# Linear attention on one core: scores and values as fp16 halves, three fp16 products for one fp32 product

## The chip, the core and the metric

The kernel runs on one NeuronCore of a Trainium2 chip. The core has a matrix engine (PE, TensorE), a vector engine (DVE), an activation engine (ACT, ScalarE), a general one (POOL, GpSimd), a queue that issues transfers (SP), an on-chip memory (SBUF, 128 partitions) and an accumulator memory for PE's results (PSUM, eight banks of 128x512 fp32). The metric is the device time of one execution in microseconds (us), as the median of some runs.

## The reference

A transformer block of six sublayers over `x` of 8 sequences x 512 tokens x 256 features in fp32. The second sublayer is the one that matters here, gated linear attention (GLA) with 4 heads, keys of 64 and values of 128 features:

```
x = x + 0.5 * ffn(layernorm(x))            # mixture of experts
x = x + gla(layernorm(x))                  # the sublayer that is changed
x = x + 0.5 * ffn(layernorm(x))
x = x + 0.5 * ternary_ffn(layernorm(x)); x = x + window_attn(layernorm(x)); x = x + 0.5 * ternary_ffn(layernorm(x))

# gla: q, k, g: [B, H, N, 64], v: [B, H, N, 128], g = log decay <= 0
S_t = diag(exp(g_t)) S_{t-1} + k_t v_t^T ;  o_t = q_t^T S_t
o = o * rsqrt(mean(o * o) + 1e-5) * rms_w
return (o.reshape(B, N, 512) * silu(x @ Wg.T)) @ Wout.T
```

## The kernel before

**Tiling.** A sequence of 512 tokens is four chunks of 128 (TPS = 4). Within a chunk the recurrence becomes a masked product: scores `att` = k q^T with the decays multiplied into q and k, masked causally, times the values. Across chunks it is a state per head, 64x128, that DVE carries on. The output of a chunk is att·v plus q·state, both accumulated in one PSUM region. Four heads are two pairs `p` of two heads `h`; half `j` of the sequence is chunks 2j and 2j+1. PE's fp16 matmuls elsewhere run in threes (`mm3`, L1701 to L1703): a value is held as an upper fp16 half and a lower fp16 half, and hi·hi, hi·lo and lo·hi are added up.

**Order.** Each engine runs a program of its own, in order; semaphores tie them. In `gla` each has a `body(g)` for sequence g; `each_sequence(..., True)` runs sequences 0 to 5 as a loop of three iterations of two, and 6 and 7 written out. PE's body: scores (L2006), transposes of the keys (L2014), the projections of the next sequence (`low`, `keys`, `logits`: L1701 to L1703 and L1978), key-value products for the states (L2030, `kt` as the stationary operand), then chunk by chunk att·v (L2042, fp32, 128 rows) and q·state (L2047, fp32, 64 rows), then the next sequence's queries and cumulated decays (L1991), the gates, the values, the turns of the gated output (L2065) with the transposes of the next rows (L1717) between them, and the output product.

**The others, around the change.** DVE masks the scores of each half from PSUM into `m.att` (L1571), then does the logits of the next sequence (L1517, L1521), the chain of states (L1562, L1565), decay (L1527), sums of squares (L1584), and the gated product (L1592). ACT copies the turned keys (L979), the low-rank rows (L949) and the keys of the next sequence (L952), does softplus (L956 to L960), the squares (L986), queries (L965), exps (L970), gates (L993), values (L975) and the upper half of the turned output (L997). PE's L2030 waits for L979, for the values and for L952, because its results go into the banks of the keys. POOL adds eps to the mean squares and raises them to -1/2 (L734, L736), scales the gates (L741), and issues an accumulating DMA of expert rows (`second_rows`, L663). `m.squares` is the same memory as `m.att`. `w1q` and `w2q` are weight buffers of a later sublayer. Before the first body, the engines work through sequence 0's projections; PE's first transposes there (L1717) wait for ACT's exps (L970).

Of the kernel before, what the change touches and what calls it, by code (L numbers as in the profile page):

```python
# [105 lines left out]
def build(nc, T, out):  # L106

    ctx = ExitStack()
    with ctx:
# [12 lines left out]
        def const(name):  # L122
            return consts[:, const_at(name)]
# [44 lines left out]
        eps = sb("eps", [P, TPS])  # L168
# [40 lines left out]
        halves_set = sem("causal_and_ones_in_half_precision")  # L209
# [18 lines left out]
        for n, kind in enumerate(SUBLAYERS):  # L228
# [7 lines left out]
                "gla": "stacked t_ready t_hi t_lo qk_ready qk_copied logits_ready lb_ready soft_step g_ready v_ready v_copied "  # L236
                       "kt_ready kt_copied cum_ready exps_ready f_step q_ready k_ready at_ready masked st_ready s_step "
                       "gate_ready gate_done gate_scaled o_ready sq_ready ss_ready orstd_step orstd_ready og_ready ogt_ready "
                       "ogt_hi ogt_lo y_ready y_taken",
                "win": "zeroed padded qk_ready qk_copied v_ready v_copied v_out v_in0 v_in1 sc_ready mx_ready "  # L240
                       "sub_ready exp_ready sum_ready rl_ready norm_ready pt_ready pt_copied c_ready ct_hi ct_lo y_ready "
                       "y_taken bias_hi bias_lo bias_product bias_row centred windowed bias_added",
# [155 lines left out]

        def gla_space():
# [16 lines left out]
            m.squares = m.att  # L416
            m.o_hi, m.o_lo = at([2, 2, 2, GPAIR, P], F16), at([2, 2, 2, GPAIR, P], F16)
# [3 lines left out]

        def flat(a):

            return a.rearrange("p a b c d -> p (a b c d)") if len(a.shape) == 5 else a.rearrange("p a b c -> p (a b c)")
# [217 lines left out]
        def _(pool):  # L642
            nc.gpsimd.memset(neghalf[:], -0.5).then_inc(rstd_step, 1)
            nc.gpsimd.memset(eps[:], EPS).then_inc(rstd_step, 1)
            pool.wait_ge(rstd_step, 2)

            def rstd_of(m):

                pool.wait_ge(mv_ready, m + 1)
                nc.gpsimd.tensor_tensor(rstd[:], mv[:, :, 1], eps[:], ALU.add).then_inc(rstd_step, 1)  # L650
# [75 lines left out]
            def gla(n):  # L726
                s, m = S[n], gla_space()
                work_left(n)

                def body(g):  # L730
                    if not is_last(g):
                        rstd_of(g + N0(n) + 2)
                    pool.wait_ge(s["ss_ready"], g * 2 + 2)
                    nc.gpsimd.tensor_tensor(m.orstd, m.ss, eps[:, 0:1, None].broadcast_to([P, 2, TPS * H // 2]), ALU.add).then_inc(s["orstd_step"], 1)  # L734
# [8 lines left out]
                    if g + 3 < NSEQ:  # L743
                        second_rows(n - 1, g + 3)

                second_rows(n - 1, 2)
                for g in range(NSEQ):
                    body(g)

            def win(n):  # L750
# [35 lines left out]
                def step(g, u):  # L786
# [10 lines left out]
                    if is_first(g):  # L797
                        pool.wait_ge(s["bias_row"], 1)
# [24 lines left out]
        def _(act):  # L823
# [120 lines left out]
            def gla(n):  # L944
                s, m = S[n], gla_space()

                def low_keys(g):
# [14 lines left out]
                def queries(g):  # L962
                    for p in range(GPAIR):
                        act.wait_ge(s["qk_ready"], g * 2 * GPAIR + GPAIR + p + 1)
                        nc.scalar.activation(m.q[:, p], ps[:, GQ[p], :], ACT.Copy, scale=DK ** -0.5 / WS).then_inc(s["qk_copied"], 1)  # L965
# [1377 lines left out]
```

## Time and profile before

| | us |
|---|---|
| median of 3 runs (1719.59 to 1725.48) | 1723.2 |
| the profiled execution | 1716.48 |
| its span, first to last instruction | 1714.4 |
| PE busy | 1638.2 (96%) |
| DVE busy | 1146.9 (67%) |
| ACT busy | 858.2 (50%) |
| POOL busy | 671.4 (39%) |
| granted TensorE clock, mean | 0.989 |

The profile is of one execution. A row of its timeline gives start, duration, engine, line of kernel.py, operation, written tile <- read tiles, shapes and how many instructions are merged into it; in square brackets, how long the engine had been idle and what ended that. A matmul's duration includes its way through the array, so matmuls overlap: what a stream costs is read from starts, or from the difference of two groups. An fp32 matmul shows as two instructions. PEld is PE's weight load, which runs beside the matmuls.

### The profile page before, as it was taken

The numbers are of one execution on the slowest core, as the hardware profiler recorded it, in microseconds if no ns is written. First come the engines' busy times: TensorE is split into PE (matmuls) and PEld (weight loads), VectorE is DVE, ScalarE is ACT, GpSimd is POOL, SyncE is SP. The second block draws the span as 40 slices with busy tenths as digits, with TensorE's granted clock in tenths as the row PEclk, the third lists the DMA queues.
The fourth block names the chain that finished last, engine by engine and source line by source line (L and its number), as shares of the span: only waits on it lengthen the run. The fifth ranks groups of instructions, "written<-read, shape, count | busy, mean of one in ns | idle before, by whom it ended". The sixth has DMA issues, their size and how long they took to land.

```text
span 1714.4 us, 41995 instructions
## 1 busy us (share of the span) xinstructions
PE 1638.2 (96%) x14962; PEld 1106.0 (65%) x14963; DVE 1146.9 (67%) x2505; ACT 858.2 (50%) x1474; POOL 671.4 (39%) x652
## 2 busy tenths in 40 slices
PE   6999999999989999999999999999999989998999
PEld 3665656666567776765565656666566767777666
DVE  6677766666556666656766656666677678776675
ACT  4455434444466555644343334444466566564774
POOL 2342333444122222123342333444244488888243
PEclk9999999999999999999999999999999999998999
DMA  7132323333302111002210123333322033221011
GB/s 249 53 110 84 97 85 98 110 106 104 84 13 38 24 25 24 1 1 84 87 50 26 37 75 96 111 108 101 96 63 48 2 76 77 54 62 40 14 37 50
DMA packets 90149, 115.69 MB, mean 67 GB/s; under 512 B 9296, under 2 KB 76400, under 8 KB 90032
## 3 DMA queue, kind: packets, MB, share of 16 engines
q1 hardware_dynamic: 69680, 71.17, 14.8%
q0 software_dynamic: 20352, 42.88, 8.8%
q8 instruction: 83, 1.36, 0.3%
q14 instruction: 34, 0.28, 0.1%
HBM read 66.11 MB, written 47.90 MB: 67 GB/s over the span
## 4 chain that ended last, share of the span: by engine, by line
PE 81%; DVE 7%; POOL 4%; ACT 4%; issue 3%; DMA 2%; SPq 0%; DVEq 0%; ACTq 0%; POOLq 0%
PE ps L1701 18%; PE ps L1703 18%; PE ps L1702 18%; PE ps L1944 3%; PE ps L1945 3%; PE ps L1717 3%; PE ps L2042 2%; PE ps L1925 2%; PE ps L1926 2%; PE ps L1863 2%; PE ps L1882 2%; PE ps L2199 2%; PE ps L2181 1%; PE ps L2169 1%; PE ps L2047 1%
## 5 line engine op out<-in xcount | busy, mean ns | idle before, releaser
L719 POOL DMA_INDIRECT routed<-work x142 | 136.5, 961 | 234.5 <-DVE work L1456 229.4
L1701 PE MATMUL ps<-later_hi,work 128*128 (+1 forms) x632 | 203.0, 321 | 1.2 <-ACT work L1054 1.0
L1702 PE MATMUL ps<-later_lo,work 128*128 (+1 forms) x632 | 203.0, 321 | 0.0
L1703 PE MATMUL ps<-later_hi,work 128*128 (+1 forms) x632 | 202.9, 321 | 0.0
L1701 PE MATMUL ps<-xt_hi,wsh 128*128 128x512 f16 x512 | 195.1, 381 | 5.3 <-DVE work L1344 3.0
L1702 PE MATMUL ps<-xt_lo,wsh 128*128 128x512 f16 x512 | 195.0, 381 | 0.0
L1703 PE MATMUL ps<-xt_hi,wsh 128*128 128x512 f16 x512 | 194.9, 381 | 0.0
L864 ACT ACTIVATE work<-ps 128x512 f32<-128x512 f32 x128 | 76.4, 597 | 182.4 <-PE ps L1703 182.1
L650 POOL TENSOR_TENSOR rstd<-mv,eps 128x4 f32<-128x4 f32 x49 | 14.7, 300 | 385.9 <-DVE mv L1149 375.1
L1701 PE MATMUL ps<-wsh,work 128*128 128x256 f16 x512 | 140.3, 274 | 4.0 <-ACT work L853 2.7
L1703 PE MATMUL ps<-wsh,work 128*128 128x256 f16 x512 | 140.4, 274 | 0.0
L1702 PE MATMUL ps<-wsh,work 128*128 128x256 f16 x512 | 140.3, 274 | 0.0
L1344 DVE SCALAR_TENSOR_TENSOR work<-ps,work 128x512 f32<-128x512 f32 x128 | 88.0, 689 | 73.7 <-ACT work L864 68.7
L1443 DVE SCALAR_TENSOR_TENSOR work<-ps,work 128x256 f32<-128x256 f32 x142 | 68.7, 484 | 98.4 <-ACT work L906 98.4
L933 ACT ACTIVATE work<-ps,cols 128x512 f32<-128x512 f32 x128 | 88.0, 687 | 64.5 <-PE ps L1926 46.3
L906 ACT ACTIVATE work<-ps 128x256 f32<-128x256 f32 x142 | 54.5, 384 | 130.4 <-PE ps L1703 128.6
L1482 DVE TENSOR_TENSOR work<-work 128x512 f16<-128x512 f32 x128 | 86.9, 716 | 43.8 <-ACT work L926 42.5
L1945 PE MATMUL ps<-w2q,work 128*128 128x256 f16 x512 | 113.3, 273 | 0.0
L1944 PE MATMUL ps<-w2q,work 128*128 128x256 f16 x512 | 113.3, 273 | 0.0
L1925 PE MATMUL ps<-xt_hi,w1q 128*128 128x512 f16 x256 | 98.1, 383 | 6.0 <-DVE xt_lo L1164 6.0
L842 ACT ACTIVATE xt_hi<-ps 128x1024 f16<-128x1024 f32 x49 | 50.1, 1023 | 101.8 <-PE ps L1717 101.8
L1926 PE MATMUL ps<-xt_lo,w1q 128*128 128x512 f16 x256 | 98.0, 383 | 0.0
(247 smaller groups left out, 4234.2 us busy)
## 6 DMA issues: line engine op xcount, KB each, us to landing
work<-expert_x SPq DMA_DIRECT2D x142, 129.0 KB, 2.1
yg<-in_w_later SPq DMA_DIRECT2D x9, 496.0 KB, 3.5
w1q<-in_w_later SPq DMA_DIRECT2D x9, 496.0 KB, 3.7
yg<-in_w SPq DMA_DIRECT2D x8, 512.0 KB, 3.6
values<-wsh SPq DMA_DIRECT2D x8, 512.0 KB, 3.3
later_hi<-values SPq DMA_DIRECT2D x16, 256.0 KB, 4.6
later_lo<-values SPq DMA_DIRECT2D x16, 256.0 KB, 4.7
out_x<-x SPq DMA_DIRECT2D x8, 512.0 KB, 3.0
```

The source lines that it names most:

```text
L719: nc.gpsimd.indirect_dma_start(routed[:, :], bass.IndirectOffsetOnAxis(m.homes[:, i:i + 1], 0), m.t_y[:, i % 4, :], None).then_inc(s[f"til ...
L864: nc.scalar.activation(m.silu[:, k % 2, :], ps[:, up_bank(g, k), :], ACT.Silu, scale=1 / WS).then_inc(s["silu_ready"], 1)
L933: nc.scalar.activation(relu[:, k % RELUS, :], ps[:, 2 + k % 4, :], ACT.Relu, bias=b1_col[:, k:k + 1]).then_inc(s["relu_ready"], 1)
L1344: nc.vector.scalar_tensor_tensor(out=m.prod[:, k % PRODS, :], in0=ps[:, up_bank(g, k) + 1, :], scalar=HS / WS, in1=m.silu[:, k % 2, :], op ...
L1482: nc.vector.tensor_tensor(h_lo[:, u, k, :], relu[:, k % RELUS, :], h_hi[:, u, k, :], ALU.subtract).then_inc(s["h_lo_ready"], 1)
L1701: nc.tensor.matmul(out_, a[0], b[0], start=start, stop=False)
L1702: nc.tensor.matmul(out_, a[0], b[1], start=False, stop=False)
L1703: return nc.tensor.matmul(out_, a[1], b[0], start=False, stop=stop)
L1925: nc.tensor.matmul(ps[:, 2 + q % 4, :], w, xt_hi[:, u, k, TOK], start=(k == 0), stop=False)
L1926: ins = nc.tensor.matmul(ps[:, 2 + q % 4, :], w, xt_lo[:, u, k, TOK], start=False, stop=(k == KT - 1))
L1944: nc.tensor.matmul(o, h_hi[:, u, q, sl], w, start=(q == 0), stop=False)
L1945: ins = nc.tensor.matmul(o, h_lo[:, u, q, sl], w, start=False, stop=(q == FU - 1))
```

## The change

After masking, the scores are split: ACT casts them to fp16 (`upper_scores`, into `a_hi`), and POOL subtracts that from the fp32 scores and writes the rest as fp16 (`a_lo`). The values are split in the same way (`upper_values` on ACT, `lower_values` on POOL), into `w1q` and `w2q`. For memory, DVE now writes the masked scores of half 0 into the room of half 1, and those of half 1 into `xn` (in the last sequence `m.lb`); the halves of j=1 are written over the fp32 scores of j=0, so ACT's cast of half 1 waits until POOL has done with half 0. On ACT the cast of half 0 stands at the head of the body, that of half 1 between the copies of the low-rank rows and the keys, and that of the next values at its end (for sequence 0 ahead of the exps). On POOL the two subtractions stand at the head of the body and that of the next values at its end. PE does, for each half, all att·v products (three of fp16 for one of fp32), waiting on `half_lo`, and then all q·state products. Queries and values are scaled by HS = 16, and eps of the output norm by HS to the fourth. Some semaphores of other sublayers are joined (`stacked`, `bias_hi` into `halves_set`; `bias_lo` into `bias_row`), which leaves their waits as they were.

```diff
+            spare = xn[:, :, 0:D]
+            rooms = [flat(m.att[:, j]) for j in range(2)]
+            m.whole = lambda g, j: (m.lb if is_last(g) else spare) if j else rooms[1].rearrange("p (a d) -> p a d", d=D)
+            halves = [a.bitcast(F16) for a in rooms]
+            m.a_hi, m.a_lo = ([a[:, n * TPS * D:(n + 1) * TPS * D].rearrange("p (h c a t) -> p h c a t", h=2, c=2, a=GPAIR)
+                               for a in halves] for n in range(2))
+            m.v_hi, m.v_lo = (a[:, :].rearrange("p (c d) -> p c d", c=TPS) for a in (w1q, w2q))
...
+                def lower_values(g):
+                    pool.wait_ge(s["half_hi"], g * 3 + 1)
+                    nc.gpsimd.tensor_tensor(m.v_lo, m.v, m.v_hi, ALU.subtract).then_inc(s["half_lo"], 1)
+
                 def body(g):
+                    for j in range(2):
+                        pool.wait_ge(s["half_hi"], g * 3 + 2 + j)
+                        nc.gpsimd.tensor_tensor(flat(m.a_lo[j]).rearrange("p (a d) -> p a d", d=D), m.whole(g, j),
+                                                flat(m.a_hi[j]).rearrange("p (a d) -> p a d", d=D), ALU.subtract).then_inc(s["half_lo"], 1)
...
                         second_rows(n - 1, g + 3)
+                    if not is_last(g):
+                        lower_values(g + 1)
 
                 second_rows(n - 1, 2)
+                lower_values(0)
...
                     act.wait_ge(s["t_ready"], g + 1)
                     nc.scalar.activation(m.t[0:3 * LOW], ps[0:3 * LOW, GLOW, :], ACT.Copy, scale=1 / WS).then_inc(s["t_hi"], 1)
+                    if between is not None:
+                        between()
                     for p in range(GPAIR):
...
+                def upper_values(g):
+                    act.wait_ge(s["v_copied"], (g + 1) * TPS)
+                    nc.scalar.activation(m.v_hi, m.v, ACT.Copy).then_inc(s["half_hi"], 1)
+
+                def upper_scores(g, j):
+                    act.wait_ge(s["masked"], g * 2 + j + 1)
+                    if j:
+                        act.wait_ge(s["half_lo"], g * 3 + 2)
+                    nc.scalar.activation(flat(m.a_hi[j]).rearrange("p (a d) -> p a d", d=D), m.whole(g, j), ACT.Copy).then_inc(s["half_hi"], 1)
 
                 def body(g, u):
+                    upper_scores(g, 0)
                     act.wait_ge(s["kt_ready"], g + 1)
...
                     if not is_last(g):
-                        low_keys(g + 1)
+                        low_keys(g + 1, lambda: upper_scores(g, 1))
                         softplus(g + 1)
+                    else:
+                        upper_scores(g, 1)
...
                     turned_hi(1)
+                    if not is_last(g):
+                        upper_values(g + 1)
...
                 queries(0)
+                upper_values(0)
                 exps(0)
...
                     for j in range(2):
                         dve.wait_ge(s["at_ready"], g * 2 + j + 1)
-                        nc.vector.tensor_tensor(flat(m.att[:, j]).rearrange("p (a t) -> p a t", t=P),
-                                                ps[:, 2 * j:2 * j + 2, :].rearrange("p a (b t) -> p (a b) t", t=P),
-                                                const("causal")[:, None, :].broadcast_to([P, 2 * H, P]), ALU.mult).then_inc(s["masked"], 1)
+                        if j:
+                            dve.wait_ge(pt_ready, g + N0(n) + 2)
+                        nc.vector.tensor_tensor(m.whole(g, j).rearrange("p a (b t) -> p a b t", t=P),
+                                                ps[:, 2 * j:2 * j + 2, :].rearrange("p a (b c t) -> p (a b) c t", t=P, b=2),
+                                                const("causal")[:, None, None, :].broadcast_to([P, H, 2, P]), ALU.mult).then_inc(s["masked"], 1)
...
-                    for c in range(TPS):
-                        if c % 2 == 0:
-                            pe.wait_ge(s["masked"], g * 2 + c // 2 + 1)
-                        if c:
+                    for j in range(2):
+                        pe.wait_ge(s["half_lo"], g * 3 + 2 + j)
+                        for c in range(2 * j, 2 * j + 2):
+                            for p in range(GPAIR):
+                                for h in range(2):
+                                    own = slice((2 * p + h) * DV, (2 * p + h + 1) * DV)
+                                    a, v = (m.a_hi[j], m.a_lo[j]), (m.v_hi, m.v_lo)
+                                    for ah, vh in ((0, 0), (0, 1), (1, 0)):
+                                        nc.tensor.matmul(ps[:, 2 * j + h, block(c, h, p)], a[ah][:, h, c % 2, p], v[vh][:, c, own],
+                                                         start=c == 2 * j and p == ah == vh == 0, stop=False, skip_group_check=True)
+                        for c in range(max(2 * j, 1), 2 * j + 2):
                             pe.wait_ge(s["s_step"], g * 5 + 2 * c - 1)
-                        for p in range(GPAIR):
-                            for h in range(2):
-                                ins = nc.tensor.matmul(ps[:, c // 2 * 2 + h, block(c, h, p)], m.att[:, c // 2, h, c % 2, p],
-                                                       m.v[:, c, (2 * p + h) * DV:(2 * p + h + 1) * DV], start=True, stop=c == 0)
-                            if c:
+                            for p in range(GPAIR):
                                 for h in range(2):
                                     rows_ = slice(h * DK, (h + 1) * DK)
-                                    ins = nc.tensor.matmul(ps[:, c // 2 * 2 + h, block(c, h, p)], m.q[rows_, p, c * P:(c + 1) * P],
-                                                           m.states[rows_, c - 1, p], start=False, stop=True)
-                        if c % 2:
-                            ins.then_inc(s["o_ready"], 1)
+                                    ins = nc.tensor.matmul(ps[:, 2 * j + h, block(c, h, p)], m.q[rows_, p, c * P:(c + 1) * P],
+                                                           m.states[rows_, c - 1, p], start=False,
+                                                           stop=c == 2 * j + 1 and p == GPAIR - 1, skip_group_check=True)
+                        ins.then_inc(s["o_ready"], 1)
```

## Rows read from the trace of the kernel before

**Rows 1.** The page: busy us of each engine, share of the span, instructions.

```profile
PE 1638.2 (96%) x14962; PEld 1106.0 (65%) x14963; DVE 1146.9 (67%) x2505; ACT 858.2 (50%) x1474; POOL 671.4 (39%) x652
```

**Rows 2.** The waits of PE, 490 to 775 us: who waited <- for whom: total us, times, longest.

```profile
PE ps L2030 <- ACT work L952: 1.8, 7, 0.3
```

**Rows 3.** The timeline of PE, L2030 of two sequences: start us, us, engine, line, operation, tiles, count.

```profile
607.75 1.53 PE L2030 MATMUL ps<-work 128*64 128x128 f32 x24 [0.25 <-ACT work L952]
...
646.62 1.53 PE L2030 MATMUL ps<-work 128*64 128x128 f32 x24 [0.25 <-ACT work L952]
```

**Rows 4.** The timeline of PE, the scores, values and turns of one sequence.

```profile
600.32 2.06 PE L2006 MATMUL ps<-work 64*128 64x128 f32 x32
...
609.21 1.60 PE L2042 MATMUL ps<-work 128*128 128x128 f32 x12
610.75 0.49 PE L2047 MATMUL ps<-work 64*128 64x128 f32 x4
611.17 0.71 PE L2042 MATMUL ps<-work 128*128 128x128 f32 x4
...
616.49 0.39 PE L1701 MATMUL ps<-xt_hi,later_hi 128*128 128x512 f16 x1
616.71 0.38 PE L1702 MATMUL ps<-xt_lo,later_hi 128*128 128x512 f16 x1
...
629.93 1.04 PE L2065 MATMUL ps<-consts,work 128*128 128x128 f32 x8
```

**Rows 5.** The timeline of PE near 189 us: fp16 matmuls of 256 columns, then of 8.

```profile
188.91 0.27 PE L1703 MATMUL ps<-wsh,work 128*128 128x256 f16 x1
189.02 0.27 PE L1701 MATMUL ps<-wsh,work 128*128 128x256 f16 x1
...
189.40 0.17 PE L1703 MATMUL ps<-wr_hi,xt_lo 128*128 128x8 f16 x1
189.43 0.17 PE L1701 MATMUL ps<-wr_hi,xt_hi 128*128 128x8 f16 x1
```

**Rows 6.** The timeline of ACT, the same sequence: the copies behind PE's products.

```profile
603.21 0.81 ACT L979 ACTIVATE work<-ps 128x768 f32<-128x768 f32 x1 [7.01 <-PE ps L2014]
...
605.80 0.60 ACT L952 ACTIVATE work<-ps 128x512 f32<-128x512 f32 x1 [0.70 <-PE ps L1703]
607.10 0.60 ACT L952 ACTIVATE work<-ps 128x512 f32<-128x512 f32 x1 [0.70 <-PE ps L1703]
```

**Rows 7.** The page's groups: a cast on ACT; busy us and mean ns after the bar.

```profile
L926 ACT ACTIVATE work<-work 128x512 f16<-128x512 f32 x128 | 78.9, 632 | 0.0
```

**Rows 8.** The timeline of DVE, 480 to 770 us: the masking of three sequences.

```profile
601.53 2.35 DVE L1571 TENSOR_TENSOR work<-ps,consts 128x1024 f32<-128x1024 f32 x2 [0.29 <-PE ps L2006]
...
640.74 2.35 DVE L1571 TENSOR_TENSOR work<-ps,consts 128x1024 f32<-128x1024 f32 x2 [0.63 <-PE ps L2006]
...
757.10 2.35 DVE L1571 TENSOR_TENSOR work<-ps,consts 128x1024 f32<-128x1024 f32 x2 [0.41 <-PE ps L2006]
```

**Rows 9.** The timeline of POOL, the same sequence: the power and the scaling.

```profile
621.62 2.94 POOL L736 TENSOR_TENSOR work<-work,neghalf 128x16 f32<-128x16 f32 x1
625.67 3.76 POOL L741 TENSOR_TENSOR work<-work 128x1024 f32<-128x1024 f32 x2 [1.12 <-ACT work L993]
```

**Rows 10.** The timeline of ACT and PE at the first sequence.

```profile
476.89 1.94 ACT L970 ACTIVATE work<-ps 128x1024 f32<-128x1024 f32 x2
...
478.92 1.58 PE L1717 MATMUL ps<-consts,xn 128*128 128x128 f32 x8 [2.85 <-issue]
```

**Rows 11.** Busy time by stretch, first sequence: PE, PEld, DVE, ACT, POOL, clock, DMA share, GB/s.

```profile
481.50:486.70 5.20, 5.12 (x40) 4.83 (x41) 3.67 (x3) 1.45 (x3) 0.00 (x0) 0.55 0.01 3
```

**Rows 12.** The timeline of all engines at the last sequence.

```profile
758.79 0.81 ACT L979 ACTIVATE work<-ps 128x768 f32<-128x768 f32 x1 [7.01 <-PE ps L2014]
...
759.70 1.53 PE L2030 MATMUL ps<-work 128*64 128x128 f32 x24 [0.95 <-issue]
```

**Rows 13.** One line's instructions on POOL, another sublayer: ns least, median, most.

```profile
L675 POOL TENSOR_TENSOR x<-x,rows x64: 716/727/2312, 1232.2 to 1701.6; 128x256 f32<-128x256 f32 x64
```

More of the change, by code:

```diff
@@ L167, in build @@
         tsum, thr = sb("tsum", [P, 2, 2]), sb("thr", [P, 2, 2])
-        eps = sb("eps", [P, TPS])
+        eps = sb("eps", [P, TPS + 1])
         neghalf = sb("neghalf", [P, 4 * TPS])
@@ L397, in l1ffn_space, with flat @@
             return r([2, FU, SEQ], F16), r([2, FU, SEQ], F16), r([RELUS, SEQ])
+        def flat(a):
+            return a.rearrange("p a b c d -> p (a b c d)") if len(a.shape) == 5 else a.rearrange("p a b c -> p (a b c)")
         def gla_space():
@@ L643, in _ @@
             nc.gpsimd.memset(neghalf[:], -0.5).then_inc(rstd_step, 1)
-            nc.gpsimd.memset(eps[:], EPS).then_inc(rstd_step, 1)
+            nc.gpsimd.memset(eps[:, 0:TPS], EPS)
+            nc.gpsimd.memset(eps[:, TPS:], EPS * HS ** 4).then_inc(rstd_step, 1)
             pool.wait_ge(rstd_step, 2)
@@ L649, in rstd_of @@
                 pool.wait_ge(mv_ready, m + 1)
-                nc.gpsimd.tensor_tensor(rstd[:], mv[:, :, 1], eps[:], ALU.add).then_inc(rstd_step, 1)
+                nc.gpsimd.tensor_tensor(rstd[:], mv[:, :, 1], eps[:, 0:TPS], ALU.add).then_inc(rstd_step, 1)
                 pool.wait_ge(rstd_step, m + 3)
@@ L733, in body @@
                     pool.wait_ge(s["ss_ready"], g * 2 + 2)
-                    nc.gpsimd.tensor_tensor(m.orstd, m.ss, eps[:, 0:1, None].broadcast_to([P, 2, TPS * H // 2]), ALU.add).then_inc(s["orstd_step"], 1)
+                    nc.gpsimd.tensor_tensor(m.orstd, m.ss, eps[:, TPS:, None].broadcast_to([P, 2, TPS * H // 2]), ALU.add).then_inc(s["orstd_step"], 1)
                     pool.wait_ge(s["orstd_step"], g + 1)
@@ L964, in queries @@
                         act.wait_ge(s["qk_ready"], g * 2 * GPAIR + GPAIR + p + 1)
-                        nc.scalar.activation(m.q[:, p], ps[:, GQ[p], :], ACT.Copy, scale=DK ** -0.5 / WS).then_inc(s["qk_copied"], 1)
+                        nc.scalar.activation(m.q[:, p], ps[:, GQ[p], :], ACT.Copy, scale=HS * DK ** -0.5 / WS).then_inc(s["qk_copied"], 1)
                 def exps(g):
@@ L974, in values @@
                         act.wait_ge(s["v_ready"], g * TPS + c + 1)
-                        nc.scalar.activation(m.v[:, c], ps[:, banks[c], :], ACT.Copy, scale=1 / WS).then_inc(s["v_copied"], 1)
+                        nc.scalar.activation(m.v[:, c], ps[:, banks[c], :], ACT.Copy, scale=HS / WS).then_inc(s["v_copied"], 1)
+                def upper_values(g):
[6 more added lines that the diff above has]
+                    nc.scalar.activation(flat(m.a_hi[j]).rearrange("p (a d) -> p a d", d=D), m.whole(g, j), ACT.Copy).then_inc(s["half_hi"], 1)
                 def body(g, u):
+                    upper_scores(g, 0)
                     act.wait_ge(s["kt_ready"], g + 1)
@@ L1071, in step @@
                                 values_rows(g + 1)
-                nc.scalar.activation(m.bv[0], bv_col, ACT.Copy).then_inc(s["bias_hi"], 1)
+                nc.scalar.activation(m.bv[0], bv_col, ACT.Copy).then_inc(halves_set, 1)
                 queries_keys(0, 0, range(2 * KT))
```

24 lines of the change are left out of this document (11 added, 13 removed).

## The prediction

> **What bounds the kernel now.** The page comes first: PE is busy 96% of the span, the next engine 67% [rows 1]. The gated linear attention (GLA) sublayer is even tighter: the waits of PE show one a sequence there, 0.3 us, for ACT's last key copy at L952 [rows 2], and the eight sequences follow each other every 38.87 us (L2030 at 607.75 and 646.62) [rows 3]. So a microsecond taken from PE's row of matmuls here is a microsecond of the kernel, as long as ACT, POOL and DVE deliver earlier by as much. The timeline of PE shows what is edited: between 609.21 and 616.49, 7.28 us, run the fp32 attention-times-values products (L2042) and the query-times-state products (L2047), alternating in fours [rows 4]. The timelines of the other engines then show what stands on either side of it.
>
> **PE's part: what is removed.** One fp32 matmul is two instructions. A group of 12 at L2042 takes 1.60 us and one of 4 takes 0.71, so one pass costs 0.89 / 8 = 0.111. The 64-row passes run two at a time: 32 of them (L2006) take 2.06, 4 (L2047) take 0.49, so one costs 1.57 / 28 = 0.056 [rows 4]. The 7.28 us hold 32 x 0.111 = 3.55 and 24 x 0.056 = 1.34. The other 2.39 fall on 12 changes between full and 64-row shapes (the ones at both ends counted as one each), 0.20 each.
>
> **PE's part: what is added.** 48 fp16 matmuls of 128 columns, each with a weight load. No such shape is in the trace. At 256 columns they start 0.11 apart, which is 256 columns at the granted 2.4 GHz (0.107) and 0.003; at 8 columns they start 0.03 apart, so load and issue together need at most that [rows 5]. For 128 columns this gives 0.0565 with the load hidden and 0.053 + 0.030 = 0.083 with it exposed. I take 0.0565, since the 256-column rows hide it. The order by kind leaves 4 shape changes. New stretch: 48 x 0.0565 + 24 x 0.056 + 4 x 0.20 = 2.71 + 1.34 + 0.80 = 4.85. PE gains 7.28 - 4.85 = 2.43 a sequence, and 1.1 with exposed loads.
>
> The Trainium skill ("TensorE: Matmul & The Clock Gate", section "Back-to-back issue gap") gives about 81 ns a matmul for a stream of loads and matmuls at 128 columns, and that would leave PE about 1.2 us of gain a sequence. The same sentence gives 131 ns for 512 columns, where this trace shows 0.22 us (616.49 to 616.71) [rows 4].
>
> **The new chain ahead of PE.** DVE masks half j=0, ACT casts it to fp16, POOL subtracts to get the lower half, and only then may ACT cast j=1, because that cast overwrites the fp32 scores of j=0. In ACT's queue the cast of j=1 stands ahead of both key copies, for which PE waits already.
> - Mask j=0: two masks take 2.35 us from 601.53, so the first ends at about 602.7 [rows 8].
> - ACT's cast of 1024 elements: from PSUM 512 take 0.60 and 768 take 0.81 [rows 6], 0.84 ns an element; 512 from SBUF to fp16 take 0.63 [rows 7]. So 1.05. It ends at 603.8 and pushes the copy at L979 from 603.21 to 603.8, which no one is near.
> - POOL's subtraction: its 1024-element TENSOR_TENSOR takes 1.9 (two in 3.76) [rows 9]. No mixed fp16 and fp32 one is shown; I take 1.9, with 1.3 and 2.9 as bounds. It ends at 605.8.
> - ACT's cast j=1: 605.85 to 606.9. The key copies then run 606.9 to 607.5 and 607.4 to 608.0, where they now run from 605.80 and 607.10 [rows 6]. PE starts L2030 at 608.05 instead of 607.75: **0.3 lost**.
> - Sequences 2 and 4, which begin a loop iteration: DVE's mask starts 0.34 later against PE (640.74 against 601.53 plus 38.87) [rows 8]; 0.65 lost.
> - Sequence 0 loses nothing, since PE's slower clock there spreads the work that covers the chain [rows 11].
>
> The second POOL subtraction runs 607.0 to 608.9, and PE needs it at about 611.9: hidden, 3 us to spare. The casts of the values (ACT 2048 elements, 1.9 us; POOL 3.8) run at about 596.3 to 602.1, where ACT is idle for 7 us [rows 6] and POOL idle; they are over 1.7 us before POOL gets the scores. If POOL were 1.5 times as slow, that cover would be gone. Softplus starts at 608.64, after the key copies, so DVE's and POOL's chains behind it stay where they are. The changed eps, the scale factors and the renamed semaphores cost nothing: the same instructions, or one memset at the start beside the loads.
>
> **What is late next.** POOL's power ends at 621.62 + 2.94 = 624.56, tied to softplus. Its scaling (1.9) would end at 626.5, DVE's product (1.2) at 627.7, and PE's first turn at L2065 is at 629.93 [rows 4, 9]. With 2.1 us gained PE comes at 627.8, just in time. So no sequence gains more than about **2.1**.
>
> **The last sequence** has no projections of a next one behind which to hide. The mask starts at 757.10 [rows 8]; cast to 759.4, L979's copy ends at 760.2 instead of 759.6, and PE's L2030 moves from 759.70 to 760.25 [rows 12]. POOL's first half is done at 761.4, the second cast at 762.5, the second subtraction at 764.5. Then 24 products, one shape change and 16 passes, 1.35 + 0.2 + 0.9 plus the hand-over, end at about 767.0 against 768.44: **1.4 gained**.
>
> **The start.** ACT casts the values of sequence 0 ahead of its exps. These run 476.89 to 478.83 and PE has been waiting for them 2.85 us when it starts at 478.92 [rows 10]. The whole 1.9 us goes on the path. PE's granted clock in the stretch behind it is 0.55, so mostly the lower level, 1.2 GHz [rows 11]; a longer wait may lengthen that stretch. If 1.9 us more work fell into it, 0.9 would be lost, and if it ended at the same moment as now, 0.9 won. I take zero.
>
> **The sum.** Sequences 0, 1, 3, 5, 6: 5 x 2.1 = 10.5. Sequences 2 and 4: 2 x (2.43 - 0.65) = 3.5. Last: 1.4. Start: -1.9. Together **13.5 us**. The profiled execution took 1716.5 (span 1714.4 and 2.1 around it), so its like should take 1703.0. The median of the runs, 1723.2, lies 6.7 above it; I carry the difference over: 1709.7.
>
> **Rivals.**
> - *The weight loads show.* 0.083 a matmul instead of 0.0565: 48 x 0.0265 x 8 = 10.2 us less gain, 3.3 left, 1719.9. For it: no stream of this width is in the trace. Against: the 256-column stream hides them. Chance 0.13. By the 81 ns of the Trainium skill the loss would be 48 x 0.0245 x 8 = 9.4 us, and the time 1719.
> - *POOL's mixed subtraction is slower, 2.9 us.* It stands on the path: 1.0 each in sequences 1 to 6, 2.0 in the last, 8 us, leaving 5.5: 1717.7. For it: L675's instruction of a quarter of the size takes 0.73 in the median, not 0.5 [rows 13]. Chance 0.15.
> - *POOL takes double, and the kernel gets slower.* At 3.8 us, the values' subtraction (7.5) ends at 605.8 and holds back the scores' by 1.8, which itself costs 1.9 more: 3.7 x 6 and 5.6 in the last, 27.8 against 13.5: 1737.5. L675 shows POOL can be held up: 0.72 at least, 2.31 at most [rows 13]. Without the queue the loss is 8 x 1.9 x (f - 1) for a factor f; from f = 1.5 on the queue adds 26 x (f - 1.5), and the two together eat the gain at about f = 1.63, 3.1 us. Against: POOL's products at L741 hold at 1.9 [rows 9]. Chance 0.10. The Trainium skill ("SBUF — State Buffer", section "Who interferes with whom") says that a DVE instruction with two SBUF inputs and a GpSimd instruction that reads SBUF exclude one another. DVE's work beside the new subtractions (masking, L1517, L1521, L1602) reads PSUM and one SBUF tile, so by that rule f stays 1. The trace agrees as far as it goes: L675's long instances run beside DVE's L1482, which has two SBUF inputs.
> - *The forecast*, 0.62, own range 1705 to 1714.
>
> **Range and chances.** The range takes in the forecast and the first two rivals with some spread between runs, not the third: 1704 to 1722. A measurement of this kernel can tell about 0.3%, 5.2 us, from no change, so "faster" is under 1718.0. The forecast and half of the second rival: 0.62 + 0.08 = 0.70. The rest of it and the first rival: 0.20. Slower: 0.10.
>
> **What would show it.** In the changed kernel: the fp16 products start 0.056 apart; the query-state products stand in blocks of 8 and 16 passes; from L2030's end to the next projections 4.85 us; PE waits about 0.6 us before L2030 for ACT's key copy, in seven sequences; POOL's 128x1024 subtraction takes 1.9 and its 128x2048 one 3.8; a sequence comes every 36.8 to 37.1 us; the first L2006 is 1.9 us later. The prediction is wrong if POOL's subtractions are much over 2 us, if the fp16 products start over 0.065 apart, or if PE waits at L2065 for DVE.

## The result, and the profile after

The changed kernel took 1717.49 us against 1724.34 us for the kernel before (medians of 12 runs each): ratio 0.9963, 95% interval 0.9951 to 0.9976, or 6.4 us less. The forecast was 13.5 us less. Its direction was right, its size over twice too large; the measured gain of 0.37% lies just above what can be told from no change. The time itself lies inside the stated range, 1704 to 1722, and outside the forecast's own, 1705 to 1714. That it is almost the 1717.7 us of the rival in which POOL takes 2.9 us is chance: the traces refute that rival.

The page of the changed kernel, busy time in us, share of the span and instructions, to be held against [rows 1]; behind it the instruction transfers from its list of queues:

```profile
span 1713.4 us, 42329 instructions
PE 1617.3 (94%) x15090; PEld 1091.3 (64%) x15091; DVE 1151.8 (67%) x2505; ACT 884.4 (52%) x1498; POOL 735.6 (43%) x677
q8 instruction: 83, 1.36, 0.4%
```

PE has 20.9 us less work, and its span is 1.0 us shorter. So nearly 20 us of what PE saved came back as idle time. One sequence in PE's timeline (start, us, engine, line, tiles, count, and in brackets the idle time before), against [rows 3, 4]:

```profile
602.16 2.06 PE L2045 MATMUL ps<-work 64*128 64x128 f32 x32
...
610.07 1.53 PE L2069 MATMUL ps<-work 128*64 128x128 f32 x24 [0.72 <-ACT work L973]
611.53 0.23 PE L2082 MATMUL ps<-w1q,work 128*128 128x128 f16 x1
611.59 0.22 PE L2082 MATMUL ps<-w2q,work 128*128 128x128 f16 x1
611.65 0.28 PE L2082 MATMUL ps<-w1q,work 128*128 128x128 f16 x2
...
612.97 0.71 PE L2089 MATMUL ps<-work 64*128 64x128 f32 x8
...
615.06 1.16 PE L2089 MATMUL ps<-work 64*128 64x128 f32 x16
616.16 0.39 PE L1740 MATMUL ps<-xt_hi,later_hi 128*128 128x512 f16 x1
...
630.06 1.09 PE L2107 MATMUL ps<-consts,work 128*128 128x128 f32 x8 [0.28 <-DVE work L1631]
```

L2045, L2069, L2082, L2089 and L2107 are the scores, the states, att·v, q·state and the turns (before: L2006, L2030, L2042, L2047, L2065). Two things are read here. The stretch from 611.53 to 616.16 is 4.63 us, where 7.28 stood. And from the scores to the states it is 7.91 us, where [rows 3, 4] give 7.43: the new chain costs 0.48. PE's waits in the GLA sublayer, 490 to 775 us (who waited, for whom: total us, times, longest), against [rows 2]. That window ends ahead of the last two turns of the kernel before, at 777.39 and 779.25, so 1.8 us of the second row, the last sequence's, stand in both kernels (1.01 and 0.76 us before):

```profile
PE ps L2069 <- ACT work L973: 5.3, 7, 1.0
PE ps L2107 <- DVE work L1631: 2.6, 5, 1.0
PE ps L2069 <- issue: 1.5, 1, 1.5
PE ps L2082 <- POOL work L745: 1.2, 1, 1.2
```

Measured from the first logits of GLA (where the sublayer's code begins to differ) to the start of the output product behind its last turn, the sublayer took 315.8 us before and 304.3 after: 11.5 us less. The rest of the difference lies elsewhere. From there to the end of the span it was 933.4 us before and 938.8 after, though none of PE's work in that part was changed. PE's waits in window attention, 1360 to 1590 us, first of the kernel before and then of the changed one:

```profile
PE ps L2181 <- POOL work L772: 12.6, 10, 2.7
PE ps L1717 <- ACT work L1030: 6.4, 7, 1.8
PE ps L2169 <- issue: 2.0, 4, 0.7
```

```profile
PE ps L2223 <- POOL work L791: 10.8, 8, 3.4
PE ps L2211 <- issue: 6.6, 5, 2.2
PE ps L1756 <- ACT work L1067: 6.4, 7, 1.8
PE ps L1741 <- issue: 3.4, 2, 1.8
```

The two rows "issue" grew from 2.0 to 10.0 us: PE stood still there, and no engine or transfer of data in the profile is what it waited for. L2211 is the same line of window attention's scores as L2169.

### The profile page after: what moved, and what is told of

The parts are those of the page before. It is cut to its first block, busy times and chain, and to the rows that moved or that the text cites. A ratio compares the mean times of both kernels' runs of the same rounds, so it can differ in the third digit from the quotient of the medians.

```text
span 1713.4 us, 42329 instructions
## 1 busy us (share of the span) xinstructions
PE 1617.3 (94%) x15090; PEld 1091.3 (64%) x15091; DVE 1151.8 (67%) x2505; ACT 884.4 (52%) x1498; POOL 735.6 (43%) x677
## 4 chain that ended last, share of the span: by engine, by line
PE 45%; DVE 5%; POOL 3%; issue 3%; ACT 2%; DMA 1%; SPq 0%; DVEq 0%; ACTq 0%; POOLq 0%
PE ps L1740 9%; PE ps L1741 9%; PE ps L1742 9%; PE ps L1983 3%; PE ps L1984 3%; PE ps L1964 2%; PE ps L1965 2%; PE ps L2241 2%; PE ps L1756 2%; PE ps L2211 2%; PE ps L2223 2%; PE ps L1921 1%; PE ps L1902 1%; ACT work L945 1%; POOL work L780 1%
## 5 line engine op out<-in xcount | busy, mean ns | idle before, releaser
L1740 PE MATMUL ps<-later_hi,work 128*128 (+1 forms) x632 | 202.6, 321 | 1.3 <-ACT work L1091 1.0
L1741 PE MATMUL ps<-later_lo,work 128*128 (+1 forms) x632 | 202.5, 320 | 0.0
L1740 PE MATMUL ps<-xt_hi,wsh 128*128 128x512 f16 x512 | 195.3, 382 | 5.6 <-DVEq L1242 2.4
L1741 PE MATMUL ps<-xt_lo,wsh 128*128 128x512 f16 x512 | 195.2, 381 | 0.0
L1740 PE MATMUL ps<-wsh,work 128*128 128x256 f16 x512 | 141.0, 275 | 3.8 <-ACT work L872 2.7
L1741 PE MATMUL ps<-wsh,work 128*128 128x256 f16 x512 | 141.2, 276 | 0.0
```

Of the source, the lines that this page charges most:

```text
L1740: nc.tensor.matmul(out_, a[0], b[0], start=start, stop=False)
L1741: nc.tensor.matmul(out_, a[0], b[1], start=False, stop=False)
```

## The experiments

Each ratio is to the kernel before, timed on the same chip, with its 95% interval. Two stretches are read from every trace: "GLA", from its first logits to the start of the output product behind its last turn, and "behind", from there to the end of the span. Each is from one trace a kernel. The kernel before has 315.8 and 933.4.

| kernel | GLA | behind | ratio |
|---|---|---|---|
| the change | 304.3 | 938.8 | 0.9963 [0.9951, 0.9976] |
| e1, the change again | 304.3 | 942.1 | 0.9966 [0.9952, 0.9980] |
| e2, order alone | 303.7 | 929.4 | 0.9916 [0.9899, 0.9933] |
| e3, values late | 302.2 | 938.9 | 0.9964 [0.9950, 0.9978] |
| e4, halves in the old order | 312.3 | 944.1 | 1.0029 [1.0010, 1.0048] |
| e5, the change + 126 | 304.7 | 929.1 | 0.9981 [0.9969, 0.9994] |
| e6, order alone + 132 | 303.1 | 943.2 | 1.0047 [1.0032, 1.0063] |
| e7, keys first + 126 | 299.6 | 930.6 | 0.9970 [0.9956, 0.9985] |
| e8, the change + 60 | 303.8 | 938.3 | 0.9934 [0.9918, 0.9950] |
| e9, keys first | 299.0 | 943.3 | 0.9958 [0.9940, 0.9977] |
| e10, keys first + 60 | 300.2 | 938.2 | 0.9924 [0.9906, 0.9942] |
| e11, order alone again | 304.0 | 930.7 | 0.9926 [0.9908, 0.9943] |

**The change again, and what each half of it does.** `e1` repeats the changed kernel beside the others.

> The changed kernel unchanged, for a second trace. Where did the missing half go? In the first trace the bodies of GLA took 14.2 us less than before and its start 2.7 more, net 11.5, but the first sublayer was 5.1 us longer and window attention about 7. Theory 'scatter': these two differ from execution to execution; then this trace has them elsewhere, and over many runs the ratio should be near 1 - 11.5/1724 = 0.9933. Theory 'code': the longer or shifted programs themselves cost issue time in window attention; then this trace shows PE's waits for 'issue' at L1740 to L1742 and L2211 again, some 8 us in all, and the ratio stays near 0.9963.

Measured: 0.9966, GLA 304.3 us, as in the first trace, with the part behind 942.1, and PE's waits for issue in window attention make 9.5 us, on the same lines. That is the theory 'code': the gain within GLA is a property of the kernel, and so is the loss behind it.

`e2` is the kernel before with only PE's order changed; the products stay fp32:

```diff
-                    for c in range(TPS):
-                        if c % 2 == 0:
-                            pe.wait_ge(s["masked"], g * 2 + c // 2 + 1)
+                    for j in range(2):
+                        pe.wait_ge(s["masked"], g * 2 + j + 1)
+                        for c in range(2 * j, 2 * j + 2):
...
```

> The kernel before, with only PE's order changed: for each half all fp32 attention-times-values products, then all query-times-state products. By the term of the sum for shape changes, 12 become 4: 8 x 0.20 = 1.6 us less a sequence in the stretch from L2042 to the next projections (7.28 to about 5.7), nothing on the other engines, so 8 x 1.6 = 12.8 us less in all, ratio 0.9926, faster than the changed kernel. Rival: the shape changes are cheap, the 7.28 us are the fp32 products themselves, and the fp16 products made the gain; then this stretch stays over 7 us and the ratio at 1.000.

Measured: 0.9916 (again as `e11`: 0.9926), faster than the change. The stretch of att·v and q·state, in `e11`'s PE timeline:

```profile
607.67 1.53 PE L2030 MATMUL ps<-work 128*64 128x128 f32 x24 [0.25 <-ACT work L952]
609.13 2.05 PE L2040 MATMUL ps<-work 128*128 128x128 f32 x16
611.11 0.71 PE L2048 MATMUL ps<-work 64*128 64x128 f32 x8
611.76 2.05 PE L2040 MATMUL ps<-work 128*128 128x128 f32 x16
613.74 1.16 PE L2048 MATMUL ps<-work 64*128 64x128 f32 x16
```

It has 5.70 us (to the next projection), 1.58 less than before; that is eight changes of shape at 0.20 each, the term of the prediction. The wait in front of it is still 0.25, for the key copy. One sequence takes 37.30 us instead of 38.87, and the sublayer is 12.1 us shorter. This is all of what the change brings there.

`e4` is the other part alone: fp16 halves, with PE's order by chunks as it was.

```diff
-                        for c in range(max(2 * j, 1), 2 * j + 2):
-                            pe.wait_ge(s["s_step"], g * 5 + 2 * c - 1)
-                            for p in range(GPAIR):
+                            if c:
+                                pe.wait_ge(s["s_step"], g * 5 + 2 * c - 1)
+                            for p in range(GPAIR):
...
```

> The changed kernel (fp16 halves, all casts and subtractions), but PE's order as before, chunk by chunk and pair by pair. By the sum it has 8 shape changes a sequence more than the changed kernel: the stretch goes from 4.63 to about 6.2 us, and the kernel takes 8 x 1.6 = 12.8 us more than the changed one, ratio to before about 1.003: the split alone gains 0.8 to 1.0 us a sequence on PE and pays 0.5 to 1.0 for the chain, 2.7 at the start and 1.5 in the last sequence. Rival (the products make the gain): stretch under 5.3 us, ratio 0.997.

Measured: the sublayer gains 3.5 us, the part behind it loses 10.7, and the ratio is 1.0029. That is the ratio expected, but by luck: GLA takes 8.0 us more than in the change, not 12.8, and the part behind makes up for it. The stretch takes 5.85 us, where 6.2 were expected and 7.28 stood before, so the eight more changes of shape cost 1.22 us here, 0.15 each, and not 0.20 as between fp32 products. The wait for ACT ahead of the stretch, which the chain through ACT and POOL makes, is as long as in the change and eats a third of the gain:

```profile
PE ps L2069 <- ACT work L973: 5.3, 7, 1.0
PE ps L2069 <- issue: 1.5, 1, 1.5
```

**The start.** `e3` is the changed kernel with ACT's cast of sequence 0's values moved behind the exps.

```diff
                 queries(0)
-                upper_values(0)
                 exps(0)
+                upper_values(0)
```

> The changed kernel with the cast of sequence 0's values behind the exps on ACT, not ahead. Expected: the 1.9 us of ACT come off the path ahead of the first body, and so does DVE's wait at L1571 (1.80 instead of 0.17 us, beside POOL's subtraction of the values), if nothing else holds: 2.7 us from the first transposes of GLA to the first scores, 30.2 to 27.5, ratio to the changed kernel 0.998. Rival: POOL's subtraction now falls beside DVE's decay products (L1578, L1579, two SBUF inputs) and holds them by up to 4 us: 28 to 31 us.

Measured: 0.9964, no change in the ratio; within its trace the stretch from the first logits to the first scores falls from 19.20 us to 16.46, the 16.47 of the kernel before. So the cast's place cost 2.7 us, not 1.9. Three rows of the changed kernel's timeline (all engines) at the first sequence, and then the one that answers in `e3`, show where the rest came from:

```profile
482.57 4.05 POOL L740 TENSOR_TENSOR w2q<-work,w1q 128x2048 f16<-128x2048 f32 x1 [14.68 <-ACT w1q L1000]
...
484.85 1.80 DVE L1571 TENSOR_TENSOR work<-work 128x6 f32<-128x6 f32 x1 [5.83 <-ACT work L991]
...
489.43 2.93 PE L2045 MATMUL ps<-work 64*128 64x128 f32 x24 [1.66 <-DVE work L1579]
```

```profile
490.69 0.17 DVE L1571 TENSOR_TENSOR work<-work 128x6 f32<-128x6 f32 x1 [4.03 <-ACT work L991]
```

DVE's tiny instruction L1571 ends at 486.65, when POOL's subtraction L740 ends at 486.62; alone it takes 0.17. DVE's L1578 and L1579 stand behind it, and PE's scores wait for L1579: counted from the first logits, L1571 starts 1.79 us later than in `e3`, which is the cast, and L1578 another 0.95 us later, the part of the 1.63 that no other wait covers. The Trainium skill ("SBUF — State Buffer", section "Who interferes with whom") says that a DVE instruction with two SBUF inputs and a GpSimd instruction that reads SBUF exclude one another; L1571 has two, and the trace agrees, with 1.80 us beside 0.17. The rival that was named for `e3` did not come: DVE's L1578 and L1579 keep their 1.23 us, and it is POOL's subtraction, issued after L1579, that takes 4.65 us there instead of 4.05. In the whole time nothing of it can be seen: 2.7 us are 0.16%, about the half width of an interval, and the GLA stretch is only 2.1 us shorter, because sequence 0 itself took 39.2 us in `e3` and 38.5 in the change (its clock is still below the full one there: 0.68 from 490 to 500 us in `e3`, 0.78 in the change).

**The part behind.** In the trace of `e1`, PE has five pauses of over a microsecond in window attention, one in each of five sequences that follow each other. The first of them, in PE's timeline:

```profile
1415.14 1.22 PE L2241 MATMUL ps<-work,later_lo 128*32 128x32 f32 x64
1416.29 0.80 PE L2211 MATMUL ps<-work,wsh 32*64 32x64 f32 x39
1418.52 0.61 PE L2211 MATMUL ps<-work,wsh 32*64 32x64 f32 x25 [1.42 <-issue]
```

The group of 64 matmuls breaks off after 39. In the next two sequences it breaks off after 48 and 57:

```profile
1443.51 0.93 PE L2211 MATMUL ps<-work,wsh 32*64 32x64 f32 x48
1446.24 0.46 PE L2211 MATMUL ps<-work,wsh 32*64 32x64 f32 x16 [1.80 <-issue]
...
1472.77 1.08 PE L2211 MATMUL ps<-work,wsh 32*64 32x64 f32 x57
1475.80 0.34 PE L2211 MATMUL ps<-work,wsh 32*64 32x64 f32 x7 [1.95 <-issue]
```

The same group of the kernel before runs through in 1.16 us:

```profile
1416.23 1.16 PE L2169 MATMUL ps<-work,wsh 32*64 32x64 f32 x64
```

The transfers of the instruction queue (q8 in the first fence) in `e1`, next to the pauses of PE that follow them, from the trace (start, duration and bytes of a transfer; end of the pause):

```
1415.84  1.13 us  16384 B   PE goes on at 1418.52, 1.55 after it landed
1443.37  1.35 us  16384 B   PE goes on at 1446.24, 1.52 after
1472.90  1.48 us  16384 B   PE goes on at 1475.80, 1.42 after
1501.64  1.37 us  16384 B   PE goes on at 1504.52, 1.51 after
1532.42  1.36 us  16384 B   PE goes on at 1535.13, 1.35 after
```

Counted in PE's own rows of the trace, from the first matmul of window attention's scores on, these pauses lie at instructions 2465, 3745, 5025, 6304 and 7584, that is 5 x 256 apart to within one instruction: a transfer of 16,384 bytes brings 256 instructions, a page, and the pauses lie on its borders. The Trainium skill ("Advanced Engine Details and Errata", section "ISA Cache") gives the same size, 16 KB or 256 instructions, and the trace agrees. It also says that there are only two such lines, beside 128 KB on TensorE. For PE the trace shows more than two: GLA's loop is 1,270 instructions long, five pages, and while its second and third iteration run (565 to 714 us in the change) the queue brings no page.

L2241 and L2211 are the densest code of PE: 128 matmuls and as many loads in some 2.4 us, about one page. PE's program has 21,364 instructions before, 116 over a multiple of 256, and 21,494 in the change, 246 over. (The queue brings 83 pages in both, and 84 when 60 or 126 are added, as these lengths would have it; the argument needs only the differences.) If the waits come from where the page borders fall, as many further instructions as bring the remainder back to 116 should take them away, and the opposite shift should bring them to a kernel that has none. `e5` and `e6` do that, with increments of a semaphore that nobody reads, at the head of PE's program:

```diff
         def _(pe):
+            for _ in range(126):
+                pe.sem_inc(stood, 1)
```

> The changed kernel with 126 semaphore increments at the head of PE's program, where PE waits 9.8 us anyway. The change made PE's program 130 instructions longer (21364 to 21494). The queue that brings instructions moves 16384 bytes at a time, 256 instructions; all four kernels with halves lost 6 to 11 us in window attention, in idle stretches of PE that end 1.3 to 1.8 us after such a transfer landed, and the order-only kernel (21362) lost none. With 126 more the window code lies as in the kernel before, modulo 256. Theory 'page': these idle stretches go, window attention takes 6 to 9 us less, ratio 0.9925 or less. Rival (the halves disturb window attention otherwise, by the joined semaphores or the state they leave): nothing moves, 0.9963.

> The order-only kernel, which lost nothing in window attention, with 132 semaphore increments at the head of PE's program: its window code then lies as in the changed kernel (21494), modulo 256. Theory 'page': it now has the idle stretches of 1.4 to 2.5 us, one a sequence, in window attention, and takes 6 to 9 us more than without, ratio 0.9955 to 0.997. Rival: ratio stays at 0.9916.

Measured, the waits of PE in window attention, of `e5` and then of `e6`:

```profile
PE ps L2226 <- POOL work L791: 12.6, 10, 3.1
PE ps L1759 <- ACT work L1067: 6.4, 7, 1.8
PE ps L2214 <- issue: 2.3, 4, 0.8
```

```profile
PE ps L2185 <- POOL work L772: 12.1, 7, 3.3
PE ps L2173 <- issue: 7.0, 4, 2.5
PE ps L1720 <- ACT work L1030: 6.4, 7, 1.8
PE ps L1705 <- issue: 2.3, 2, 1.5
```

The part behind GLA falls from 942.1 to 929.1 in the first, and rises from 929.4 to 943.2 in the second. Of these 13.0 and 13.8 us, 10.4 and 8.1 fall in window attention, whose times are given with `e8` below; the others fall elsewhere and were not traced to a cause, but for a pause of 1.9 us at L1795 that `e1` has at 813 us and `e5` has not. Nothing but the increments at the head tells these pairs apart, and both kernels start about 10 us later by them, the one to go faster behind and the other slower: it is the length, not the delay. The ratios (0.9981, 1.0047) missed what was expected (0.9925 or less, 0.9955 to 0.997) and say less than the stretches: the increments themselves take time, some 0.16 us each, and PE's first matmul starts at 20.19 us in `e5` where it started at 9.76:

```profile
20.19 1.94 PE L1759 MATMUL ps<-consts,xn 128*128 128x128 f32 x8 [20.19 <-issue]
```

`e8` therefore takes 60, which fit into those 9.8 us (PE starts at 10.11).

> The changed kernel with 60 increments of a semaphore at the head of PE's program: half of the shift that 126 gave, and at some 0.16 us each (about 9.5 us) just inside the 9.8 us that PE is idle at the start, so they should cost nothing. Theory (the place of the code's 16 KB pages decides the waits in window attention): the stretch behind GLA, 938.8 us unpadded and 929.1 with 126, lies at one of the two or between them; a gradual dependence gives some 933 and a ratio to before near 0.992, all or nothing gives 0.990 or 0.9965. Rival (the 126 worked by something else, such as the later start): no fall behind GLA, ratio 0.9965.

Measured: 0.9934. In its trace the part behind takes 938.3 us, hardly less than in the change, as the rival had it. But the pauses have moved: up to 1490 us none is over a microsecond, and the last three sequences have one each, 1490 to 1590 us,

```profile
PE ps L2226 <- POOL work L791: 6.2, 4, 3.0
PE ps L2214 <- issue: 5.5, 3, 2.1
```

Neither "all or nothing" nor "gradual" describes it. What does is where the borders fall. Window attention is not a loop; its eight sequences are written out, 1,262 PE instructions each, 18 short of five pages, so in each sequence every border falls 18 instructions (9 matmuls with their loads: 39, 48, 57 above) later in the code than in the one before. Take all 13 traces together, leave out the first two sequences (where the change and `e3` have one pause of 1.1 us), and count each border's place from the start of the first of a sequence's four groups of scores (L2169, and the same line elsewhere):

| place of the border in a sequence's code | kernels that have one there | pause at it |
|---|---|---|
| 394 to 454 | the change, e1, e3, e4, e6, e9 (sequences 2 to 5); e8, e10 (5 to 7) | 1.4 to 2.7 us, all 30 times |
| 472 | the change, e1, e3, e4, e6, e9 (sequence 6) | 0 to 1.6 us |
| everywhere else | all | at most 1.0 us; in 26 of 341 cases over 0.25 |

The kernel before, `e2`, `e11`, `e5` and `e7` have no border from 367 to 529. Window attention, from its first scores to its last products with the values, takes 216.9 us before and 215.8, 218.1, 215.9 and 216.2 in these four; 224.0, 226.3, 223.5, 226.5, 224.0 and 226.3 in the change, `e1`, `e3`, `e4`, `e6` and `e9`; 220.2 and 223.4 in `e8` and `e10`. The costly place is the second half of the second group of scores and the beginning of the projections (L1740, L1741) behind it.

The ratio of `e8` came out lower than the two stretches give: against before they make 12.0 - 4.9 = 7.1 us, 0.4%, and the timing says 0.5 to 0.8%. And `e8` loses 4.7 us to `e5` ahead of window attention, near 1020 us, where it waits longer for a data transfer and its granted clock is 0.66 for 10 us instead of 1.00; "behind" holds such scatter too.

**The chain.** PE waits for L973, the key copies, which stand behind the second cast in ACT's queue. `e7` puts them ahead of it (with the values late, and 126 increments); `e9` is the same without increments, `e10` with 60.

```diff
-                    if between is not None:
-                        between()
                     for p in range(GPAIR):
...
+                    if between is not None:
+                        between()
```

> The changed kernel with three edits: the 126 increments, the cast of the first values behind the exps, and ACT's cast of score half 1 behind the key copies instead of ahead. The last takes the chain mask, cast, subtraction, cast off the way to PE's L2069: it should start 7.43 us after the scores again instead of 7.9 to 8.2. Expected if the chain was the cost: 0.5 to 0.75 us less in sequences 1 to 6. Rival: the next wait, PE's first turn for DVE's gated product, takes it over in the odd sequences (they stay at 37.2) and only sequences 2, 4 and 6 gain. GLA in all 14 to 17 us under before, ratio 0.990 to 0.992: at or just under the order-only kernel.

> The changed kernel with the values of sequence 0 behind the exps and ACT's cast of the second half behind the key copies, without increments; PE's program as long as that of the changed kernel. Within GLA 299.6 us between its first logits and its last turn, as with the 126 increments (304.3 in the changed kernel). Theory: the stretch behind GLA is 938 to 942 as in the changed kernel, since PE's code is the same; time 4.7 us under the changed kernel, ratio to before 0.994. Rival (the waits of window attention depend on something else than PE's code): 930, ratio 0.989.

> The same with 60 increments at the head of PE's program. If the stretch behind GLA falls to about 930 as with 126 increments and the 60 are hidden at the start, 16 us under before's GLA minus nothing elsewhere: ratio 0.990, below the order alone (0.9916). If 60 do not move the stretch behind GLA, 0.994.

Measured in GLA: 299.6, 299.0 and 300.2 us. The scores to the states take 7.43 us again. But only every second sequence profits: the periods of `e9` alternate, 37.21 and 36.23, where the change has 37.2 and 37.0. Its waits in GLA:

```profile
PE ps L2107 <- DVE work L1631: 4.1, 5, 1.0
PE ps L2069 <- ACT work L971: 1.8, 7, 0.3
PE ps L2069 <- issue: 1.5, 1, 1.5
```

Of the 3.5 us that the wait for ACT gave back, 1.5 went into the wait for DVE's gated product at the turn. The rival named for `e7` is what came: the odd sequences stay at 37.2. Its ratio, 0.9970, missed the 0.990 to 0.992 by the 10 us that PE starts later. The ratios of the others are 0.9958 and 0.9924: with all the pauses in window attention, and with those of the last three sequences only (behind 943.3 and 938.2, where 930 was hoped for in `e10`). `e10` and the order alone, timed side by side (0.9924 and 0.9926), cannot be told apart, and both are faster than the change.

## Why the prediction was half right

**The direct costs of PE held.** The fp16 products start 0.056 us apart (611.53, 611.59, 611.65), the value taken from the 256-column rows; the rival in which the weight loads show is refuted. The Trainium skill ("TensorE: Matmul & The Clock Gate", section "Back-to-back issue gap") has 81 ns for such a stream; the measurement decides for 56. The stretch was forecast at 4.85 us and has 4.63. The 0.20 us for a change of shape, inferred from a remainder, was confirmed by `e2` for fp32 products: its stretch leaves 0.20 for each of four changes. Beside fp16 products a change costs 0.15, by the same sum, with 12 of them in `e4` (5.85) and with 4 in the change (4.63); that is the missing 0.22. So of the 2.65 us of gain 1.58 come from the order alone and 1.43 from the halves alone, which overlap by 0.36.

**The chain was under-sized by a little.** Its mechanism is as told: cast, subtraction, cast, key copies. POOL's 1024-element subtraction takes 2.13 and 2.06 us instead of the 1.9 taken, inside the bounds of 1.3 and 2.9 and without any long instance. PE loses 0.47 (forecast 0.3) in the odd sequences, 0.77 (0.65) in 2 and 4, and 0.50 in 6. The rivals in which POOL takes 2.9 or 3.8 us are refuted.

**The cap held, with one exception.** "No sequence gains more than about 2.1" was tied to DVE's product at the turn. Sequences 1 to 5 gain 1.7 to 1.9 and sequence 6 gains 2.15. PE waits at the turn for 0.3 us in three of them, which the prediction had named as a sign of being wrong; it came just in time, as forecast, and a little too early. `e9` shows that this wait takes up what is gained ahead of it. Sequence 0 gains 2.47, but its length is not steady: `e9` and `e10`, alike but for the increments, have 37.9 and 39.1 us for it. In the last sequence the gain is 0.87 and not 1.4: both subtractions lie on the path there and take 2.13 each, 0.46 of the missing 0.53. Together the bodies from the first scores on gain 14.2 us; forecast were 15.4.

**The start was under-sized**: 2.7 us and not 1.9. The cast's duration was right, but its consequence, POOL's subtraction of the values beside DVE's chain, was left out. The prediction named the very rule, and applied it only to DVE's instructions in the middle of a sequence.

Up to here the forecast, -13.5, stands against -11.5 in the traces.

**The step that failed is the last of the sum**: that what lies outside GLA stays as it is ("its like should take 1703.0"). No term stood there, and no rival. The runs put one of 5 to 10 us in its place: window attention takes 216.9 us before and 224.0 and 226.3 in the two traces of the change, by pauses of PE at page borders. Each of the four bodies in PE's program (two in the loop, two written out) got 16 more matmuls and 16 more loads, 128 in all, and with two more waits it is 130 longer; from there on every page border falls elsewhere, in window attention into the place where it costs.

In three traces of kernels with this length (the change, `e1`, `e3`) the part behind GLA is 5.4, 8.7 and 5.5 us longer than before; `e9` has 9.9. With the mean, 7.4, the sum is -11.5 + 7.4 = -4.1; measured are -6.4, with an interval from -8.4 to -4.1. The same sum for the order alone, -12.1 - 4.0 = -16.1, stands against a measured -14.3; for `e4`, -3.5 + 10.7 = +7.2 against +5.0. So the two stretches explain the times to about 2 us. What they leave is what lies ahead of GLA: the first logits came at 465.1 us in the one trace of the kernel before, and at 469.1 to 477.9 in those of all kernels with no increments, though PE's work up to there is the same in all. That the profiled execution was 6.7 us faster than the median fits this scatter, though one trace does not show it; the change's profiled execution was 2.2 us faster than its median.

**Still open.** That the pauses lie at page borders, that the length of the program decides, and in which place of the code a border costs is shown. Why it costs there, and not in the three other groups of scores, is not: the code ahead of that place is dense, 256 instructions in some 2.4 us, and each pause of over 0.9 us ends 1.2 to 1.8 us after its page has landed, but when a page is asked for does not show in the traces. The order alone is 2.7 to 4.0 us faster behind GLA than the kernel before, whose remainder is almost the same (114 and 116). In window attention it is not (215.8 and 218.1 against 216.9), so that difference is no matter of these borders; it may be scatter, since the kernel before has one trace.

## What to carry to other kernels

Take a change apart before you pay for all of it: here the reordering alone, which costs no other engine anything, gives as much in the sublayer as reordering and fp16 halves together. When PE's products become cheaper at the price of a cast and a subtraction on other engines, look up which copies stand behind them in those queues, and put what PE waits for first. And after every edit compare the stretches that the edit does not touch. Waits for "issue" that appear there were here a matter of the program's length, and took back about half of the gain. Look whether they are a multiple of 256 instructions apart; some instructions more or less, in a place where the engine waits anyway, then show it.

## What was unexpected in the hardware

- The length of PE's program alone changes the time of unchanged code behind it by 13 to 14 us in 930 (`e1` to `e5` 942.1 to 929.1; `e2` to `e6` 929.4 to 943.2), 10.4 and 8.1 us of it in window attention, mostly by pauses of 1.3 to 2.7 us that end some 1.5 us after a 16,384-byte instruction transfer has landed, at borders of 256 instructions.
- PE holds more than two pages of 256 instructions: GLA's loop of 1,270 brings no transfer in its second and third iteration.
- An increment of a semaphore on PE takes some 0.16 us (126 of them 20 us), three times as long as one of the fp16 products.
- A change between full-array and 64-row matmuls costs PE 0.20 us when both are fp32 (1.6 us a sequence for twelve against four), and 0.15 when the full-array ones are fp16.
- POOL's subtraction with an fp16 input and an fp16 output takes 2.06 to 2.13 us for 1024 elements and 4.07 for 2048, where the fp32 product of the same size takes 1.9.
- A DVE instruction of six elements took 1.80 us instead of 0.17 beside POOL's subtraction.
